# Six-row exponent products in row groups by batch and head parity, three transfers a side for their rows, and the experts' low halves made inside the mLSTM loop

## The reference

```python
def _mlstm_head(q, k, v, ig, fg):
    log_fg = jax.nn.log_sigmoid(fg)
    cs = cumsum of log_fg, with a zero ahead
    log_D = where(lower triangle, cs[1:, None] - cs[None, 1:], -inf) + ig.T
    max_log_D = jnp.max(log_D, axis=-1, keepdims=True)
    D = jnp.exp(log_D - max_log_D)
    qk = q @ (k.T / sqrt(DH))
    C = qk * D
    normalizer = jnp.maximum(jnp.abs(C.sum(-1, keepdims=True)), jnp.exp(-max_log_D))
    return C / (normalizer + EPS) @ v
# q = layernorm(x), k = v = ctx, ig and fg = [q, k, v] @ (gate kernels) + biases
```

## Time and profile before

| what | us |
|---|---|
| three timed runs | 611.39, 608.80, 612.28 |
| median of them | 611.39 |
| the profiled execution, whole | 608.86 |
| its span, first to last instruction | 607.1 |

### The profile page before, as it was taken

How to read it: one execution, slowest core, us unless ns; L and a number is a source line. 1 busy time by engine, 2 the same in 40 slices (tenths; PEclk the granted TensorE clock), 3 DMA queues, 4 the chain that set the end, 5 groups by cost and what they waited for, 6 DMA issues and landing times. The chain is left out here.

```text
span 607.1 us, 15295 instructions
## 1 busy us (share of the span) xinstructions
PE 463.7 (76%) x5721; PEld 351.2 (58%) x5721; DVE 449.0 (74%) x1027; ACT 380.6 (63%) x705; POOL 218.0 (36%) x203
## 2 busy tenths in 40 slices
PE   6266699999999999999998674441899506599996
PEld 5254677777777777787787523330555303356664
DVE  7976877878687787869867598962354587888886
ACT  4674587887877888787774477150667514545553
POOL 2630633242333324233332144156566562710000
PEclk9669899999999999999999965555555556899999
DMA  9106000000000000000000050041000000000000
GB/s 222 62 1 146 9 3 2 3 1 0 0 0 0 1 3 2 0 0 0 0 2 1 12 96 0 2 79 40 1 2 2 1 0 1 0 2 19 18 17 17
DMA packets 19405, 11.64 MB, mean 19 GB/s; under 512 B 10040, under 2 KB 17296, under 8 KB 19360
## 3 DMA queue, kind: packets, MB, share of 16 engines
q1 hardware_dynamic: 18528, 10.34, 7.5%
q0 software_dynamic: 768, 0.70, 0.6%
q10 hardware_dynamic: 64, 0.00, 0.0%
HBM read 6.64 MB, written 1.05 MB: 13 GB/s over the span
## 5 line engine op out<-in xcount | busy, mean ns | idle before, releaser
L824 POOL TENSOR_TENSOR gprob<-gprob 128x512 f16<-128x512 f32 x64 | 74.9, 1170 | 147.3 <-ACT gprob L1038 147.0
L1038 ACT CAST gprob<-gprob 128x512 f16<-128x512 f32 x64 | 39.7, 621 | 27.5 <-DVE gprob L1133 27.5
L1126 DVE TENSOR_REDUCE negmax<-psM 128x4 bf16<-128x512 f32 x64 | 43.6, 683 | 17.1 <-PE psM L881 17.1
L1133 DVE SCALAR_TENSOR_TENSOR gprob<-psG,prob 128x512 f32<-128x512 f32 x64 | 44.0, 688 | 14.7 <-ACT prob L1072 7.1
L903 PEld LDWEIGHTS psG<-kron,emb 128*128 128x128 f16 x768 | 48.9, 99 | 9.5 <-issue 0.3
L903 PE MATMUL psG<-kron,emb 128*128 128x128 f16 x768 | 54.0, 220 | 0.0
L1935 DVE SCALAR_TENSOR_TENSOR cmat<-psMS,decay 128x512 f32<-128x512 f32 x32 | 20.6, 686 | 40.1 <-ACT decay L1905 27.9
L1837 POOL TENSOR_TENSOR cmat<-cmat 128x512 f16<-128x512 f32 x32 | 36.3, 1157 | 24.7 <-ACT cmat L1910 24.7
L1072 ACT ACTIVATE prob<-psS 128x512 f32<-128x512 f32 x64 | 34.6, 592 | 14.0 <-PE psS L895 13.9
L925 PE MATMUL aux<-woT,attT 128*128 128x128 f32 x256 | 32.8, 281 | 12.3 <-ACT qT L1020 11.5
L891 PE MATMUL psS<-qT,kT 64*128 64x128 f32 x512 | 37.2, 285 | 3.1 <-DVE negmax L1126 1.6
(11 more groups left out here) (364 smaller groups left out, 1242.8 us busy)
## 6 DMA issues: line engine op xcount, KB each, us to landing
kS<-ctxT SPq DMA_DIRECT2D x24, 64.0 KB, 2.3
qS<-qT SPq DMA_DIRECT2D x16, 64.0 KB, 2.3
out_dram<-x_sb SPq DMA_DIRECT2D x4, 256.0 KB, 2.3
raw<-in_L_xattn_Wq_dram SPq DMA_DIRECT2D x1, 512.0 KB, 10.4
raw<-in_L_xattn_Wk_dram SPq DMA_DIRECT2D x1, 512.0 KB, 8.3
raw<-in_L_xattn_Wv_dram SPq DMA_DIRECT2D x1, 512.0 KB, 6.7
raw<-in_L_xattn_Wo_dram SPq DMA_DIRECT2D x1, 512.0 KB, 6.2
w<-in_L_ffn_w_dram SPq DMA_DIRECT2D x2, 256.0 KB, 2.9
```

The lines of the kernel that those rows point to most:

```text
L824: nc.gpsimd.tensor_tensor(gprob2[:, u % 2, 1], gprob[:, u % 2], gprob2[:, u % 2, 0], ALU.subtract).then_inc(gplo_ready, 1)
L1038: nc.scalar.copy(gprob2[:, u % 2, 0], gprob[:, u % 2]).then_inc(gphi_ready, 1)
L1126: v.tensor_reduce(negmax[:, u % 2], psM[u % 2][:], AX.X, ALU.max, negate=True).then_inc(negmax_ready, 1)
L1133: v.scalar_tensor_tensor(out=flat(gprob[:, u % 2]), in0=flat(psG[:]), scalar=1e-6 * G_UP, in1=flat(prob[:, u % 2]), op0=ALU.max, op1=ALU.m ...
```

## The change

The 128 (batch, head) places of the gates are ordered anew: first by the parity of the batch, then by the parity of the head, then by head pair j and batch pair c. A block of 32 partitions now holds one combination of the two parities.

- The 12 + 12 row transfers become 3 + 3. Each takes one bf16 part of all 128 partitions and writes four partitions, 32 apart, 32 x 128 elements each. All six signal two semaphores, `peak_in` and `gain_in`; the exponents of batch 0 wait for all of them, where the first four batches each waited for their own six.
- The eight 6-row products of a batch run with the head group inside: groups 0 and 1 alternate, and read from partitions 32 apart. Group 0 is signalled with the seventh product of the eight instead of the fourth.
- The order of the gate biases is turned once (`gb_turned`, a DVE copy that DVE waits for). The gates' additions go from two instructions of 128 columns to four of 64, and the maximum with `eguard` from one to two.
- The low halves of the experts' weights leave the end of the preparation block and are issued on DVE in the loop after the work of batches 3, 6, 9 and 12.

```diff
-    def row_of(a, k, row):
-        at = 32 * k + row
-        return a[at:at + 1].rearrange("o b h q -> o (b h) q")
+    def rows_of(a, row):
+        return a[row:row + 97:32].rearrange("k j b q -> k (j b) q")
...
-            for k in range(4):
-                for part in range(NSPLIT):
-                    sp.dma_start(row_of(rowX, k, part), peak3[32 * k:32 * k + 32, part]).then_inc(peak_in[k], 16)
+            for part in range(NSPLIT):
+                sp.dma_start(rows_of(rowX, part), peak3[:, part]).then_inc(peak_in, 16)
...
-            for k in range(4):
-                for part in range(NSPLIT):
-                    pool.dma_start(row_of(rowW, k, NSPLIT + part),
-                                   gain3[32 * k:32 * k + 32, part]).then_inc(gain_in[k], 16)
+            for part in range(NSPLIT):
+                pool.dma_start(rows_of(rowW, NSPLIT + part), gain3[:, part]).then_inc(gain_in, 16)
...
-                if b < 4:
-                    pe.wait_ge(peak_in[b], 16 * NSPLIT)
-                    pe.wait_ge(gain_in[b], 16 * NSPLIT)
-                for g in range(G):
-                    n = G * b + g
-                    for j in range(GH):
-                        mm = mm_(psA[n % RING][:, j], rowW[at:at + 2 * NSPLIT, b // 4, 2 * j + g],
...
-                    mm.then_inc(a_psum, 1)
+                if b == 0:
+                    pe.wait_ge(peak_in, 16 * NSPLIT)
+                    pe.wait_ge(gain_in, 16 * NSPLIT)
+                for j in range(GH):
+                    for g in range(G):
+                        at = 32 * (2 * (b % 2) + g)
+                        mm = mm_(psA[(G * b + g) % RING][:, j], rowW[at:at + 2 * NSPLIT, j, b // 2],
...
+                        if j == GH - 1:
+                            mm.then_inc(a_psum, 1)
...
+            def low_weights(n):
+                raw, hi, lo = expert_halves(later)[n]
+                dve.wait_ge(later["moe_hi"], n + 1)
+                v.scalar_tensor_tensor(out=lo, in0=raw, scalar=W_UP, in1=hi, op0=ALU.mult,
+                                       op1=ALU.subtract).then_inc(later["moe_lo"], 1)
...
+                if b in LOW_AT:
+                    low_weights(LOW_AT.index(b))
```

More of the change, by code:

```diff
@@ L1621, in mlstm_phase @@
     gk2 = sb("gk2", [P, 2, 3, 2 * H1], F16, scope)
-    gates = sb("gates", [P, 2, B, H1], F32, scope)
+    gates = sb("gates", [P, 2, 2, 2, GH1, HALF], F32, scope)
+    gb_turned = sb("gb_turned", [P, 2, H1], F32, scope)
     low = sb("low", [P, P], F32, scope)
@@ L1733, in _ @@
             act.wait_ge(guard_psum, 1)
-            nc.scalar.activation(eguard[:].rearrange("p b h -> p (b h)"), psE[:], ACT.Exp,
+            nc.scalar.activation(eguard[:].rearrange("p s r j c -> p (s r j c)"), psE[:], ACT.Exp,
                                  scale=-1.0).then_inc(eg_ready, 1)
@@ L1745, in _ @@
                                    op1=ALU.subtract).then_inc(gk_ready, 1)
+            order.then(v.tensor_copy(gb_turned[:].rearrange("p k (r j) -> p k r j", r=2),
+                                     gb[:].rearrange("p k (j r) -> p k r j", r=2)))
             layernorm_all(v, steps, 3, order, dve, B - 4, bnst, mv, rstd)
@@ L1757, in _ @@
             for k in range(2):
-                v.scalar_tensor_tensor(out=gates[:, k], in0=psI[:, :, k], scalar=1.0 / W_UP,
-                                       in1=gb[:, k].unsqueeze(1).to_broadcast([P, B, H1]), op0=ALU.mult,
-                                       op1=ALU.add).then_inc(gates_ready, 1)
+                for odd in range(2):
+                    v.scalar_tensor_tensor(out=gates[:, k, odd].rearrange("p r j c -> p c (r j)"),
+                                           in0=psI[:, HALF * odd:HALF * odd + HALF, k].rearrange("p c r j -> p c (r j)"),
+                                           scalar=1.0 / W_UP, in1=gb_turned[:, k].unsqueeze(1).to_broadcast([P, HALF, H1]),
+                                           op0=ALU.mult, op1=ALU.add).then_inc(gates_ready, 1)
             dve.wait_ge(gatesT_psum, 1)
@@ L1777, in _ @@
                     order.then(v.tensor_tensor(peak[:], peak[:], peak3[:, part], ALU.subtract))
[L1779 to L1782, removed]
         @block.tensor
@@ L1790, in gate_products @@
                 for x_part, w_part in PARTS:
[L1791 removed]
+                    mm = mm_(psI[:, place(b)], src[:, x_part, b],
+                             gk2[:, w_part, s].rearrange("p (k j r) -> p k r j", k=2, r=2),
                              start=(b == 0 and s == 1 and x_part + w_part == 0),
@@ L1811, in _ @@
             mm.then_inc(gate_psum, 1)
-            pe.wait_ge(gates_ready, 2)
+            pe.wait_ge(gates_ready, 4)
             for k in range(2):
-                mm = nc.tensor.transpose(psF[:, k], gates[:, k].rearrange("p b h -> p (b h)"), ident[:])
+                mm = nc.tensor.transpose(psF[:, k], gates[:, k].rearrange("p s r j c -> p (s r j c)"), ident[:])
             mm.then_inc(gatesT_psum, 1)
@@ L1966, in _ @@
                                               op0=ALU.mult, op1=ALU.max))
-            order.then(v.tensor_tensor(factor[:].rearrange("p (j k) h -> p j k h", k=4),
-                                       factor[:].rearrange("p (j k) h -> p j k h", k=4),
-                                       eguard[:].rearrange("p (k j) h -> p j k h", k=4), ALU.max))
+            for odd in range(2):
+                fs = factor[:, odd::2].rearrange("p c (j r) -> p c j r", r=2)
+                order.add(v.tensor_tensor(fs, fs, eguard[:, odd].rearrange("p r j c -> p c j r"), ALU.max))
+            order.sync()
             order.then(v.tensor_scalar(factor[:], factor[:], 1e-6, None, ALU.add))
```

17 lines of the change are left out of this document (8 added, 9 removed).

## The result

| | median, us | runs, us |
|---|---|---|
| before | 610.61 | four runs, 608.80 to 612.28 |
| after | 603.28 | four runs, 602.34 to 604.57 |

The ratio is 0.988, with a 95% interval from 0.985 to 0.992. The forecast was 603.3. The profiled execution of the changed kernel took 604.57, with a span of 602.8.

The account below looks back on a forecast made before the run. POOL's path was taken to set the loop's start, and a chain of 7.01 us per two batches to bound the loop. Terms -4.3 - 3.1 + 0.2 + 0.1 - 3.4 + 3.0 = -7.5 from 610.8 gave 603.3 us, range 599.5 to 607.8.

Parts of the forecast that it names:

- The sum: Whole kernel: the predicted terms added up, -7.5 us, taken against a mean of 610.8 us; chance 0.45.
- bias copy and gates: Ahead of the normalisation: copy of 16 bias columns and the wait for it, +0.2 us; the split gate additions 0.
- low halves leave the preparation: Preparation block: POOL's five short instructions, no longer beside DVE's, take 1.97 us instead of 5.06, -3.1.
- POOL's issues: End of preparation: POOL issues 3 row transfers instead of 12, 1.6 us against 5.93, -4.3.
- from the last issue to the mask products: End of preparation: landing stays 1.7 to 2.1 us after the issue, so no change in the sum, 0.
- 6-row products, eight periods: Loop: eight alternating products take 0.54 us instead of 0.96, 0.42 less in each of eight periods, -3.4 us.
- low halves in the loop: Loop, batches 3, 6, 9: DVE delays POOL's second subtraction about 1.4 us; +3.0 after TensorE's slack, bounds +0.3 to +4.1.
- tail: Loop's tail: the second maximum and its gap stand on the path, +0.1 us.
- The rival: End of preparation: four-partition transfers land late, at 6.0 us, delaying rows or the block's end; 605.4 to 607.6 us, chance 0.22.
- a fixed time after the last issue or a wait for the landing: Preparation's end: two open explanations for most of the 2.49 us between POOL's last issue and TensorE's first loop product.
- the rival without collision: Loop: DVE's low halves and POOL's subtractions don't delay each other; -10.2 us, 600.6 us in all, chance 0.12.
- The opposing terms: Loop: -3.4 us from 6-row products against +3.0 from low halves, length about unchanged; the gain is POOL's path ahead.

Follow-up runs that it names:

- held-back kernel: Changed kernel with the experts' low halves back at the preparation's end, behind a wait for POOL's last gain split: 601.25 us, measured again 599.86 us, ratio 0.984 both times.
- the last kernels: The held-back kernel again (599.86 us), and, with ACT issuing the gain's transfers, two low halves at the loop's head (603.60 us) or all four (601.34 us).

## Why the prediction came out right, step by step

The sum was -7.5. The medians differ by 7.3 and the profiled mLSTM stages by 6.44. The time was right with terms that were not all right, and that it came out as close as 0.02 us is luck.

| step | predicted | measured | where |
|---|---|---|---|
| bias copy and gates | +0.2 | +0.28 | POOL's first split 19.16 into the block, then 19.44 |
| low halves leave the preparation | -3.1 | -3.03 | first split to first issue 5.35, then 2.32 |
| POOL's issues | -4.3 | -3.78 | 5.93, then 2.15 |
| from the last issue to the mask products | 0 | +1.26 | 2.49, then 3.75 |
| 6-row products, eight periods | -3.4 | -3.58 | loop without low halves, 56.84, against 60.42 |
| low halves in the loop | +3.0 | +2.24 | 59.08 against 56.84 |
| tail | +0.1 | +0.17 | 13.41, then 13.58 |

*The transfers* were mis-sized: 2.5 us of gain in place of 4.3 (3.0 with the shorter landing that two other kernels with the same transfers had). This is the step that failed. Half a us is the issue, 0.71 each where I took 0.50 to 0.58. The rest is the landing, which I left at "1.7 to 2.1" in the sum and gave 0.22 as a rival. The rival had both halves of the mechanism: the late landing, and the end of the block that follows it. Only its price of 6.0 us was too high; 3.5 was measured. With POOL as issuer the mask products followed the last landing by about a us: 1.3 before (421.9 to 423.19), 0.9 in the held-back kernel (its last issue, at 413.3, landed 3.1 later, and the mask products came at 417.33). In the five profiled executions with three transfers issued by POOL the last landed between 2.7 and 3.5 us after its issue, and the mask products came 0.93 behind the landing each time. With twelve they came 1.3 behind it in all four executions, with six 1.06. With ACT they did not follow it. That is what I had left open between "a fixed time after the last issue or a wait for the landing": for POOL's transfers it behaves as the wait.

*The low halves in the loop.* The mechanism was the one foretold, DVE and POOL in turn, and so the rival without collision fell. The Trainium skill, "SBUF — State Buffer", section on the engines' ports ("Who interferes with whom"), has a DVE instruction with two SBUF inputs and a GpSimd one that reads SBUF shut each other out; the pair of 3.39 and the DVE instruction of 2.19 agree with it. The size was 1.12 each time and not 1.4, since POOL's first subtraction had begun before DVE came and was not interrupted: only the second waited. And I had 0.2 pushed over to the other chain where nothing was. Twice 1.12 on the odd chain (batches 3 and 9) is the 2.24 measured; batch 6 cost the even chain 1.1, which the odd one, with the last batch on it, never saw. On the kernel before, where the 6-row products take longer, the odd chain does get 0.3 of batch 6, which makes 2.54.

*The 6-row products* came as forecast, 0.54 for eight and a period of 6.62, but for a reason that I had given only in part. I had compared them to the scores, which alternate, and took the order as part of it. The order plays no part; the groups of partitions do. And the gain is 0.40 for a period and comes nine times on the way through the loop, not 0.42 eight times.

*The opposing terms.* The forecast said that the loop would stay about as long as it was and the gain would be POOL's path in front of it. In fact the loop gained 1.34 and the preparation 5.27. The two errors, +1.8 for the transfers and -0.8 for the low halves, partly cancel, and the stages together are 1.1 short of the sum. That the medians differ by 7.3 and not 6.4 is within their interval (a ratio of 0.985 to 0.992 is 5 to 9.5 us).

## What to carry to other kernels

Fewer and larger transfers save issue time, but the price is read from the landing as well as from the issues: when they are the last of a block, the later landing can take back a third of what the issues save (1.26 of 3.78 here). That the landing grew because few partitions are written is not shown: the twelve, which write one partition each, landed soonest. Work that collides with an engine on the critical path is best put where that engine only issues transfers or waits for them, which here was worth 2.2 us more than moving it into a loop. Products with a contraction of 6 overlapped when their operands lay in different groups of partitions and their results in different buffers; it costs a layout, not an order.

## What the runs showed of the hardware

- The end of a block followed the landing of POOL's transfers by 0.93 to 1.3 us in ten profiled executions, and did not wait for those of ACT, whose rows landed 2 us behind the block's end.
- ACT's first issue took longer than the two behind it in each of three kernels: one of 1.36 to 1.42 us and two of 0.54. With POOL as issuer the three took 0.77, 0.71 and 0.68.
- DVE and POOL computing in SBUF took turns; DVE computing and POOL issuing transfers did not (2.15 us for three issues in both cases).
- The profiled executions differ before they reach the change. The kernel before has runs near 609, 611.5 and 614.5 us; which part of it differs between them was not recorded. The window from 50 to 100 us, in code common to all kernels here, shows a difference in the granted clock (the number behind POOL's count): first the kernel with two low halves at the loop's head, whose mLSTM stage began at 395.77, then the held-back kernel's second run, where it began at 389.86.

```profile
50.00:100.00 50.00, 41.37 (x555) 34.17 (x556) 32.67 (x61) 31.09 (x64) 16.83 (x14) 0.90 0.21 48
```

```profile
50.00:100.00 50.00, 42.42 (x611) 35.20 (x610) 35.93 (x70) 34.54 (x71) 19.51 (x17) 0.97 0.22 48
```

TensorE did 555 products in one and 611 in the other. In the profiled executions with 0.97 there the stage began between 389.9 and 393.3, in those with 0.90 or 0.91 between 392.4 and 395.8. The two ranges overlap, so this window is not the whole of it. The starts lie up to 6 us apart, more than the 1.3 by which the last kernels differ, so a stage is compared by its own length. Whether one kernel meets the later start more often than another was not tried.
